# One more wait ahead of a down-projection step: TensorE begins down step 2 of a group only after the group's last gate and up job has ended

## The chip, the cores and the metric

The kernel runs on one core of one Trainium2 chip. The metric is the device time of one execution in microseconds (us), the median over several runs. TensorE (PE in the profile) multiplies matrices and loads their weights (PEld), VectorE (DVE) and ScalarE (ACT) do element-wise work, GpSimd (POOL) does more of it, SyncE (SP) only issues transfers. Engines run their own instruction streams in order and meet at semaphores.

## The reference, cut to what matters

A block on 16,384 tokens (8 sequences of 2048) of 256 features: a layer norm, linear attention with a residual and a second norm, a gated feed-forward network with a third norm, and a ternary-weight gate on the result.

```python
xn = _layernorm(x)
qkv = xn @ Wqkv + bqkv; q, k, v = split(qkv)
qp, kp = elu(q) + 1, elu(k) + 1
kv = einsum('bsd,bse->bde', kp, v)
attn = (qp @ kv) / (qp . sum(kp) + ATTN_EPS)
z = layer_norm(xn + attn, g1, b1)
gate, up = z @ Wg + bg, z @ Wu + bu          # 256 -> 682
ffn = (silu(gate) * up) @ Wd + bd            # 682 -> 256
s = layer_norm(z + ffn, g2, b2)
out = x + s * silu(xn @ ternary(weight).T)
```

## The kernel before, in words

The tokens are cut into 32 groups of 512. An iteration of the main loop works on several groups at once: on group f = i the feed-forward network, on q = i + 1 the attention output, on a = i + 5 the keys and values. Every float is split into a high and a low part, so that one product takes three matmuls: high by high, and the two cross terms (`parts3`).

TensorE's work is a hand-written list of jobs for an iteration, `TENSOR_JOBS` (line 90); `END_JOBS` (line 111) is the list of the last group. The names that matter here are G and U (gate and up of one of five 128-wide slices of the hidden layer, six matmuls with 512 columns each), GU 5 (the remainder of gate and up in one job, six matmuls), D 0 to D 5 (the down product of one slice into the two `d_bank` buffers, twelve matmuls with 256 columns; D 5 has four), K and Q (keys and queries), KV (once in four iterations), N (attention output), B (the ternary product), and XK. The list of a middle iteration ends in `XK 1, XK 2, XK 3, GU 5, D 2, TZ 0, TZ 1, D 3`, where the two TZ jobs are left out for all groups from 1 to 30; it begins with `K 0, D 4, KV 0, KV 1, D 5, K 1, N 0`. So the job GU 5 stands directly ahead of D 2. In the list of the last group D 2 comes ahead of U 4 and of GU 5.

Each job begins with its waits. A job that writes one of the five rotating banks waits first until that bank is free, then for its own inputs. `Dn`, the function of the D jobs, waits for the semaphore `hl`, which VectorE raises when the slice of the hidden layer has its high and low parts. GU 5's last matmul raises the semaphore `GU`. ScalarE waits on it for the silu of the remainder (line 811), and ScalarE's copy of the next group's `zT_h` waits on it too (line 802). The hidden parts lie in a ring of three buffers, `h_h` and `h_l`; ScalarE refills a slot when the D job three slices earlier has ended.

The loops of ScalarE, VectorE and GpSimd have lists of the same kind (lines 93 to 109). VectorE takes K's result in `k_add` (line 1014), the attention output in `attn` (lines 1048 to 1058), the hidden layer in `h_rows` and `h_low` (lines 1095 and 1105), and the down result in `ffn_rows` (line 1117). Its `kv_low` (line 1172) releases job N after job KV.

Of the kernel before, what the change touches and what calls it, by code (L numbers as in the profile page):

```python
# [46 lines left out]
GROUPS = BATCH * SEQ // TOK  # L47
# [165 lines left out]
def build_kernel(nc, x, wqkv, bqkv, wg, bg, wu, bu, wd, bd, g1, b1, g2, b2, wt, out):  # L213
# [10 lines left out]
    with ctx:  # L224
# [3 lines left out]
        def sem(name):  # L228
            return ctx.enter_context(nc.semaphore(name))
# [103 lines left out]
        S = {n: sem("s_" + n) for n in names}  # L333

        def parts3(hi_l, lo_l, hi_r, lo_r):

            return ((hi_l, hi_r), (lo_l, hi_r), (hi_l, lo_r))
# [929 lines left out]
        def _(eng):  # L1267
            def products(dst, pairs, name, first=True, last=True, **kw):

                for n, (left, right) in enumerate(pairs):  # L1270
                    ins = eng.matmul(dst, left, right, start=first and n == 0,  # L1271
                                     stop=last and n == len(pairs) - 1, **kw)
                if name:
                    ins.then_inc(S[name], 1)
# [109 lines left out]
            def Dn(g, c):  # L1384
                eng.wait_ge(S["hl"], HC * g + c + 1)
                if c == 0:
                    eng.wait_ge(S["r2"], PAIRS * g)
                    if g == 0:
                        eng.wait_ge(S["w_dl"], 1)
                        eng.wait_ge(S["w_dt"], 1)  # L1390
                if c == HF:
                    eng.wait_ge(S["ha"], 2 * (g + 1))
                slot = (HF * g + c) % HRING
                for t in range(TILES):
                    s = slice(t * P, (t + 1) * P)
                    if c < HF:
                        pairs = parts3(h_h[:, slot, s], h_l[:, slot, s], wd_h[:, c, :], wd_l[:, c, :])
                    else:
                        pairs = ((ht[:, s], wd_h[:, c, :]),)

                    products(d_bank[t // 2][:, (t % 2) * D:(t % 2 + 1) * D],
                             pairs, "D" if t == TILES - 1 or (g == GROUPS - 1 and c == HF and t % 2) else None, first=c == 0 and t % 2 == 0,
                             last=c == HC - 1, skip_group_check=True)
# [38 lines left out]
            for i in ITERATIONS:  # L1442
                for kind, g, n in schedule(i):
                    if kind == "XK":
                        XK(g, n)
                    elif kind == "D":
                        Dn(g, n)
                    elif kind in setup:
                        setup[kind]()
                    else:  # L1450
                        number = NUMBER[kind, g, n]
                        if number >= RING:
                            stage_, count = freed(*JOBS[number - RING])
                            eng.wait_ge(S[stage_], count)
                        run[kind](g, n, bank[number % RING])
# [24 lines left out]
```

## Time and profile before

| | |
|---|---|
| median of three runs | 1210.11 us (1208.1 to 1210.26) |
| the profiled execution's own time | 1209.84 us |
| its span in the profile | 1208.1 us |
| busy: TensorE matmuls, VectorE, ScalarE, GpSimd | 1187.2, 1079.5, 953.2, 843.7 us |
| mean granted TensorE clock | 0.998 of full |

The busy time of TensorE runs from the start of a matmul to its modelled end, and matmuls overlap: one with 512 columns is shown as 0.39 us long, but the next starts about 0.23 us after it. So the distance between starts is the pace, and the shown duration is what a reader of the result has to wait for. A stretch can have no idle time in the record and still run later than its pace.

### The profile page before, as it was taken

The page shows a single profiled execution, that of the slowest core. Times are in us where ns is not written, and L with a number is a line of the kernel's source. Part 1 is how long each engine was busy: PE and PEld are TensorE (multiplying, and loading weights), DVE is VectorE, ACT ScalarE, POOL GpSimd, SP SyncE. Part 2 cuts the span into 40 slices and gives each one's busy share as a digit, 9 for nine tenths or more (in the row PEclk, how much of TensorE's full clock was granted, in tenths as well). Part 3 has the DMA queues.
Part 4 walks back from the last instruction along what each step waited for, and adds up shares of the span by engine and source line. Part 5 has one row for each costly group of instructions (what it writes and reads, how often), then busy time and mean ns, then how long its engine had stood idle before and what let it go on. Part 6 is the DMA issues. An engine that isn't in the chain of part 4 may idle for free.

```text
span 1208.1 us, 24021 instructions
## 1 busy us (share of the span) xinstructions
PE 1187.2 (98%) x7550; PEld 1067.3 (88%) x7550; DVE 1079.5 (89%) x2467; ACT 953.2 (79%) x1557; POOL 843.7 (70%) x994
## 2 busy tenths in 40 slices
PE   8999999999999999999999999999999999999997
PEld 6889998989988999988989989899988999888886
DVE  6988999999999999999999999999999999777765
ACT  7787888878888888888878888788887878867753
POOL 3443787767787776787757887677886767766676
PEclk9999999999999999999999999999999999999999
DMA  7213432334432334432334432244332343222201
GB/s 216 78 48 88 123 106 70 88 106 123 123 104 72 88 106 123 122 105 73 88 106 122 110 103 83 75 123 123 109 96 67 97 123 105 71 71 63 76 21 36
DMA packets 137523, 115.61 MB, mean 96 GB/s; under 512 B 12339, under 2 KB 122293, under 8 KB 137398
## 3 DMA queue, kind: packets, MB, share of 16 engines
q1 hardware_dynamic: 137398, 114.08, 32.6%
q8 instruction: 62, 1.02, 0.3%
q14 instruction: 63, 0.52, 0.1%
HBM read 67.38 MB, written 46.67 MB: 94 GB/s over the span
## 4 chain that ended last, share of the span: by engine, by line
PE 52%; DVE 21%; ACT 11%; issue 9%; DMA 3%; POOL 2%; SPq 1%; DVEq 0%; ACTq 0%; POOLq 0%
PE bank L1271 36%; PE d_bank L1271 11%; PE xk_bank L1271 5%; DVE st L922 3%; DVE bank L1095 3%; ACT rz L695 3%; DVE rz L1054 2%; DVE h_l L1105 2%; DMA xa<-z_turned 2%; DMA z_turned<-xa 2%; ACT h_h L695 1%; DVE zT_l L1085 1%; ACT ku L695 1%; POOL norm L569 1%; ACT hs L695 1%
## 5 line engine op out<-in xcount | busy, mean ns | idle before, releaser
L1271 PE MATMUL bank<-zT_h,wgu_h 128*128 128x512 f32 x704 | 275.1, 391 | 1.1 <-DVE rz L1054 1.1
L1271 PE MATMUL bank<-zT_l,wgu_h 128*128 128x512 f32 x704 | 275.1, 391 | 0.0
L1271 PE MATMUL bank<-zT_h,wgu_l 128*128 128x512 f32 x704 | 275.0, 391 | 0.0
L695 ACT ACTIVATE rz<-rz,norm 128x256 f32<-128x256 f32 x252 | 140.5, 595 | 53.6 <-DVE norm L1131 53.6
L569 POOL TENSOR_TENSOR norm<-ve,consts 128x4 f32<-128x4 f32 x64 | 72.9, 1139 | 154.7 <-DVE ve L933 154.5
L1271 PE MATMUL d_bank<-wd_h,h_h 128*128 128x256 f32 x640 | 179.4, 280 | 0.1
L1271 PE MATMUL d_bank<-wd_h,h_l 128*128 128x256 f32 x640 | 179.2, 280 | 0.0
L1271 PE MATMUL d_bank<-wd_l,h_h 128*128 128x256 f32 x640 | 179.2, 280 | 0.0
L1095 DVE SCALAR_TENSOR_TENSOR bank<-bank,hb,hs 128x512 f32<-128x512 f32 x160 | 117.9, 754 | 53.6 <-ACT hs L695 41.9
L695 ACT ACTIVATE h_h<-bank 128x512 fp32r<-128x512 f32 x160 | 95.7, 598 | 80.7 <-DVE bank L1095 80.4
L1271 PEld LDWEIGHTS bank<-zT_l,wgu_h 128*128 128x128 f32 x704 | 132.2, 188 | 28.1
L1271 PEld LDWEIGHTS bank<-zT_h,wgu_h 128*128 128x128 f32 x704 | 132.4, 188 | 25.6 <-DVE rz L1054 3.9
L695 ACT ACT_TABLE_LOAD x116 | 148.8, 1283 | 4.0 <-POOL wd_l L678 1.2
L1271 PEld LDWEIGHTS bank<-zT_h,wgu_l 128*128 128x128 f32 x704 | 132.2, 188 | 20.1
L592 POOL TENSOR_TENSOR ksum<-ksum,kp 128x256 f32<-128x256 f32 x120 | 108.3, 903 | 45.6 <-DVE kp L1021 42.3
L695 ACT ACTIVATE hs<-bank,hb 128x512 f32<-128x512 f32 x192 | 128.3, 685 | 13.2 <-PE bank L1271 12.2
L1105 DVE TENSOR_TENSOR h_l<-bank,h_h 128x512 fp32r<-128x512 f32 x160 | 110.0, 687 | 23.7 <-ACT h_h L695 17.5
L1271 PEld LDWEIGHTS d_bank<-wd_h,h_h 128*128 128x128 f32 x640 | 120.2, 188 | 3.1 <-DVE h_l L1105 0.5
L1271 PEld LDWEIGHTS d_bank<-wd_h,h_l 128*128 128x128 f32 x640 | 120.2, 188 | 2.7
L1271 PEld LDWEIGHTS d_bank<-wd_l,h_h 128*128 128x128 f32 x640 | 122.2, 191 | 0.0
L642 POOL TENSOR_TENSOR rz<-rz,g1b 128x256 f32<-128x256 f32 x128 | 118.1, 933 | 0.0
L602 POOL TENSOR_TENSOR rz<-rz,g2b 128x256 f32<-128x256 f32 x124 | 90.6, 741 | 34.9 <-ACT rz L695 34.9
(163 smaller groups left out, 3571.8 us busy)
## 6 DMA issues: line engine op xcount, KB each, us to landing
xq<-in_L_attn_x_dram SPq DMA_DIRECT2D x32, 512.0 KB, 5.9
xa<-in_L_attn_x_dram SPq DMA_DIRECT2D x31, 512.0 KB, 3.9
out_dram<-rz SPq DMA_DIRECT2D x31, 512.0 KB, 5.0
z_turned<-xa SPq DMA_DIRECT2D x120, 128.0 KB, 3.3
xa<-z_turned SPq DMA_DIRECT2D x30, 512.0 KB, 4.1
turned<-xa SPq DMA_DIRECT2D x108, 128.0 KB, 2.4
xa<-turned SPq DMA_DIRECT2D x27, 512.0 KB, 3.9
rz<-in_L_attn_Wg_dram SPq DMA_DIRECT2D x1, 640.0 KB, 5.7
```

The lines of the kernel that those rows point to most:

```text
L569: eng.tensor_tensor(dst, ve[:, k, :], neg_half[:, 0:1].to_broadcast([P, TILES]), ALU.pow).then_inc(S[f"rs{k}"], 1)
L592: eng.tensor_tensor(ksum[:, slot, :], ksum[:, slot, :], part, ALU.add).then_inc(S["ks"], 1)
L602: eng.tensor_tensor(row_, row_, g2b[:, :], ALU.mult).then_inc(S["a"], 1)
L642: eng.tensor_tensor(row_, row_, g1b[:, :], ALU.mult).then_inc(S["zg"], 1)
L695: return eng.activation(out_, in_, func, **kw).then_inc(S[name], 1)
L922: eng.bn_stats(st[:, k, t, :], rows).then_inc(S[f"bn{k}"], 1)
L1054: eng.scalar_tensor_tensor(out=rz[:, g % RZ, t, :], in0=num[:, 0:D], scalar=den[:, n % 2, 1:2], in1=rz[:, g % RZ, t, :], op0=ALU.mult, op1 ...
L1085: eng.tensor_tensor(to, source, high.bitcast(f32), ALU.subtract).then_inc(S["zTl"], 1)
L1095: eng.scalar_tensor_tensor(out=hidden(g, c)[0:rows, :], in0=up, scalar=hb[0:rows, HC + c:HC + c + 1], in1=hs[0:rows, n % 2, :], op0=ALU.ad ...
L1105: eng.tensor_tensor(h_l[:, slot, :], hidden(g, c)[:, :], h_h[:, slot, :].bitcast(f32), ALU.subtract).then_inc(S["hl"], 1)
L1271: ins = eng.matmul(dst, left, right, start=first and n == 0, stop=last and n == len(pairs) - 1, **kw)
```

## The change

In `Dn` a third wait is put in for step c = 2 of every group but the last. It wants the semaphore `GU` at g + 1, so that group g's remainder job has ended. No instruction is moved and none is taken away; the step now has the wait for `hl` first and the wait for `GU` second.

```diff
@@ -1390,6 +1390,8 @@
                         eng.wait_ge(S["w_dt"], 1)
                 if c == HF:
                     eng.wait_ge(S["ha"], 2 * (g + 1))
+                if c == 2 and g < GROUPS - 1:
+                    eng.wait_ge(S["GU"], g + 1)
                 slot = (HF * g + c) % HRING
                 for t in range(TILES):
                     s = slice(t * P, (t + 1) * P)
```

The place in TensorE's stream, once in each of the 31 groups from 0 to 30. Ahead of it stand the last two matmuls of GU 5, behind it the first three of D 2.

```order
 L1271 MATMUL bank<-zT_h,wgu_l 128x512
 L1271 MATMUL bank<-zT_l,wgu_h 128x512
-L1271 MATMUL d_bank<-wd_h,h_h 128x256 [waits s_hl]
+L1271 MATMUL d_bank<-wd_h,h_h 128x256 [waits s_GU,s_hl]
 L1271 MATMUL d_bank<-wd_h,h_l 128x256
 L1271 MATMUL d_bank<-wd_l,h_h 128x256
```

Nothing moved: the first matmul of D 2 has one more semaphore to wait for, and that semaphore is raised by the matmul right above it. VectorE, ScalarE, GpSimd and SyncE have the same rows as before.

## Rows read from the trace of the kernel before

**Rows 1.** The page: span, busy time, and the chain that ended last by engine
```profile
span 1208.1 us, 24021 instructions
PE 1187.2 (98%) x7550; PEld 1067.3 (88%) x7550; DVE 1079.5 (89%) x2467; ACT 953.2 (79%) x1557; POOL 843.7 (70%) x994
...
PE 52%; DVE 21%; ACT 11%; issue 9%; DMA 3%; POOL 2%; SPq 1%; DVEq 0%; ACTq 0%; POOLq 0%
```

**Rows 2.** Timeline (start us, length us) at D 2 of group 13
```profile
574.45 0.39 PE L1271 MATMUL bank<-zT_l,wgu_h 128*128 128x512 f32 x1
...
574.68 0.28 PE L1271 MATMUL d_bank<-wd_h,h_h 128*128 128x256 f32 x1
...
574.80 0.28 PE L1271 MATMUL d_bank<-wd_h,h_l 128*128 128x256 f32 x1
```

**Rows 3.** Timeline: GU 5's last matmul of group 14, and ScalarE's silu
```profile
610.16 0.39 PE L1271 MATMUL bank<-zT_l,wgu_h 128*128 128x512 f32 x1
...
610.59 0.69 ACT L695 ACTIVATE hs<-bank,hb 62x512 f32<-62x512 f32 x1
```

**Rows 4.** Timeline at N 0 of group 12, whose late wait is not its first
```profile
474.20 0.43 DVE L1172 TENSOR_TENSOR kv_l<-bank,kv_h 128x258 fp32r<-128x258 f32 x1
...
474.75 0.19 PEld L1271 LDWEIGHTS bank<-kv_h,qp_h 128*128 128x128 f32 x1 [0.24 <-issue]
474.78 0.36 PE L1271 MATMUL bank<-kv_h,qp_h 128*128 128x258 f32 x1
...
474.97 0.28 PE L1271 MATMUL bank<-kv_h,qp_l 128*128 128x258 f32 x1
```

**Rows 5.** Timeline at Q 1 of group 13, whose late wait is its first
```profile
487.67 0.68 DVE L1105 TENSOR_TENSOR h_l<-bank,h_h 128x512 fp32r<-128x512 f32 x1
...
488.40 0.19 PEld L1271 LDWEIGHTS bank<-xT_h,wq_h 128*128 128x128 f32 x1 [0.34 <-DVE h_l L1105]
488.40 0.50 PE L1271 MATMUL bank<-xT_h,wq_h 128*128 128x512 f32 x1
...
488.75 0.40 PE L1271 MATMUL bank<-xT_h,wq_l 128*128 128x512 f32 x1
```

**Rows 6.** Timeline: first matmul of D 2 in groups 0, 1, 14, 15, 26
```profile
102.52 0.28 PE L1271 MATMUL d_bank<-wd_h,h_h 128*128 128x256 f32 x1
...
138.17 0.28 PE L1271 MATMUL d_bank<-wd_h,h_h 128*128 128x256 f32 x1
...
610.39 0.28 PE L1271 MATMUL d_bank<-wd_h,h_h 128*128 128x256 f32 x1
...
649.07 0.28 PE L1271 MATMUL d_bank<-wd_h,h_h 128*128 128x256 f32 x1
...
1048.40 0.28 PE L1271 MATMUL d_bank<-wd_h,h_h 128*128 128x256 f32 x1
```

**Rows 7.** Timeline: first matmul of KV 0, and D 5 behind KV 1
```profile
616.30 0.28 PE L1271 MATMUL bank<-wv_h,kv_h 128*128 128x256 f32 x1
...
618.08 0.48 PE L1271 MATMUL d_bank<-wd_h,ht 128*128 128x256 f32 x2
```

**Rows 8.** Waits of 102 to 1048 us by engine: us in total, times, longest
```profile
PEld bank L1271 <- DVE h_l L1105: 4.6, 15, 0.7
...
PEld bank L1271 <- DVE rz L1054: 2.5, 10, 0.6
PEld bank L1271 <- issue: 2.3, 8, 0.5
```

**Rows 9.** Timeline: K 1's last matmul of group 19, VectorE's `k_add`
```profile
582.10 0.28 PE L1271 MATMUL bank<-wk_l,xT_h 128*128 128x256 f32 x1
...
582.83 0.67 DVE L1014 TENSOR_TENSOR kp<-bank,bk1b 128x512 f32<-128x512 f32 x1
```

**Rows 10.** One stretch: us, busy per engine, granted clock (PEclk) behind POOL
```profile
102.50:1048.40 945.90, 944.52 (x6077) 855.55 (x6076) 884.19 (x1990) 779.43 (x1264) 701.81 (x805) 1.00 0.34 100
```

**Rows 11.** Timeline: weight load of U 0 in group 29, after a wait
```profile
1122.03 0.19 PEld L1271 LDWEIGHTS bank<-zT_h,wgu_h 128*128 128x128 f32 x1 [1.33 <-DVE rz L1054]
```

## The prediction

> **What bounds the kernel now.** I read the page's busy times first: TensorE is busy 98% of the span, VectorE 89% [rows 1]. Busy time alone does not show who sets the pace, because shown matmuls overlap, so I went to the distances between starts. D 2 begins once in an iteration, and its first matmul is a good clock: 102.52, 138.17 and so on to 1048.40 us [rows 6]. The shortest distance is 35.65 us, and it holds when all of TensorE's jobs follow each other without a break. If all 26 iterations between 102.52 and 1048.40 were like it, with 1.78 us more for each of the six that hold the KV jobs (616.30 to 618.08 [rows 7]), the stretch would take 26 x 35.65 + 6 x 1.78 = 937.6 us. It takes 945.9. So TensorE sets the pace, but loses about 8.3 us to stalls, 0.3 us an iteration. They are not spread evenly. Taking the same bases, 16 of the 26 distances are at most 0.23 us over, about 0.9 us together; the other ten are 0.42 to 1.34 us over. The longest is 610.39 to 649.07 [rows 6], a KV iteration.
>
> What TensorE waits for in those is VectorE: `h_low`, `attn`, and the late `kv_low` that the view of waits books as "issue" [rows 8]. So VectorE's chain is second and close behind, and that matters for the sum.
>
> The two chains meet at one place in each iteration. GU 5's last matmul starts at 610.16 and ends at 610.55; ScalarE's silu of it starts at 610.59, 0.04 us later [rows 3]. That is one of 23 such pairs (groups 3 to 25); the gap is 0.04 in most and 0.19 us at most. From there ScalarE and VectorE go their own way until they release TensorE again in K, N, Q or U.
>
> **The price of one pause.** Today D 2 follows GU 5 without a break: starts at 574.45, 574.68 and 574.80 [rows 2], with D 2's first weights loaded under the last matmul of GU 5. With the wait, TensorE must see that matmul end. I take the steps one by one.
>
> End of the matmul: 0.39 us after its start [rows 2]. From the end of a releaser to TensorE's next weight load: VectorE's `kv_low` ends at 474.63, the load starts at 474.75, which is 0.12; the matmul starts 0.03 after the load and the second matmul 0.19 after the first, at 474.97 [rows 4]. When the late wait is the first of its job it is quicker: `h_low` ends at 488.35 and load and matmul both start at 488.40, 0.05 later, though the second matmul comes 0.35 after the first where the usual pace is 0.23 [rows 5]. The new wait stands behind the one for `hl`, which is like the job N, whose late wait is also behind another; I take that case. Then D 2's second matmul, the first that is back on the normal pace, starts at 574.45 + 0.39 + 0.12 + 0.03 + 0.19 = 575.18 in place of 574.80. One pause costs 0.38 to 0.39 us. By the quicker case it would be 0.39 (end) + 0.05 (release) + 0.12 (0.35 - 0.23, the second matmul's delay) - 0.23 (the distance of today) = 0.33. No row shows TensorE waiting for itself; the other end of a wait for TensorE, ScalarE's 0.04 us [rows 3], is no longer than the 0.05 seen from VectorE, so I see no reason for a dearer signal, and allow 0.45 as the upper bound.
>
> There are 31 pauses, one for each group from 0 to 30: 31 x 0.39 = 12.1 us. Behind the waiting matmul stand, in TensorE's stream, D 2, D 3 and all of the next iteration. The instructions of the other engines are unchanged, and what they wait for from D 2 (the ring of hidden slots, the banks) is used many microseconds later. The wait itself is fulfilled the moment the drained matmul is signalled; there is nothing else to wait for.
>
> **What of it is hidden.** The pause lies behind GU 5, and the chain ScalarE - VectorE starts from GU 5, not from D 2. So in an iteration where TensorE later stalls for VectorE, TensorE only arrives later at a place where it would have stood anyway, and the pause costs nothing up to the length of the stall. This needs VectorE not to be late in turn. The tightest place that I found where it takes something from TensorE behind the pause is `k_add` of K 1: K 1's last matmul starts at 582.10 and ends at 582.38, `k_add` starts at 582.83, 0.45 later [rows 9]. Less the 0.04 of the signal there is a margin of 0.41 us, and the pause of 0.39 just fits in. I take the hand-overs of the other jobs (K 0, D 5, N, G, U) as looser.
>
> Ten iterations have stalls of over 0.39 us, so they hide ten pauses. The 1.33 us gap ahead of U 0 in group 29 [rows 11] hides an eleventh. That is 11 x 0.39 = 4.3, and of the small stalls I count 0.4 of the 0.9 us. Hidden: 4.7 us, as much as 12 whole pauses. Net: 12.1 - 4.7 = 7.4 us. The profiled execution took 1209.84 us, so 1217.2; the median of the runs is 0.27 above it, which gives **1217.5 us**.
>
> **The rivals.**
>
> *Nothing is hidden.* If the margin at `k_add` does not hold, or VectorE's chain moves along with TensorE for another reason, the stalls stay and every pause counts. For it: the margin is only 0.02 us larger than the pause. Against it: at N 0 of group 12 the stall ends with VectorE's `kv_low` [rows 4], on a chain that began at GU 5, ahead of the pause. Time: 1210.1 + 12.1 = 1222.2.
>
> *The pause is smaller.* With the weights of D 2 loaded while the wait is open, the first matmul would come 0.43 us after the last one's start and the next at the normal pace, 0.20 us lost: (31 - 12) x 0.20 = 3.8, or 1213.9. Against it: in both waits that I read the load starts only after the releaser [rows 4, 5]. The middle case of 0.33 gives 19 x 0.33 = 6.3, or 1216.4, and belongs to my forecast. The Trainium skill, page "TensorE: Matmul & The Clock Gate", section "Step-by-step: what each phase is for", says that the engine pulls the next weight load ahead of matmuls in flight; if a load could also pass a wait, this rival would hold. The rows show the pulling ahead at D 2 today (the load of its first weights is not on the path [rows 2]), and none past a wait.
>
> *Not slower: VectorE and ScalarE set the period.* If their chain from one GU 5 to the next took as long as TensorE's, TensorE would have at least 0.39 us to spare in every iteration, and the pauses would go into it: 1210.1, at most 1211. It decides from a spare time of 0.39 us in each of the 26. For it: VectorE is busy for 884 of 945.9 us [rows 10], and the chain that ended last has only 52% of TensorE in it [rows 1]. Against it: 16 of 26 distances have no more than 0.23 us to spare, and silu waits for GU 5 in each [rows 3]. So the pause must show in those 16.
>
> *The clock falls.* The stretch ran at a granted clock of 1.00, which is 2.4 GHz [rows 10], and the 1.33 us gap [rows 11] did not lower it. If a short pause in each iteration did bring the lower level, 1.2 GHz, for no more than D 2, its twelve matmuls of 0.12 us (574.68 to 574.80 [rows 2]) would take 1.4 us more: 31 x 1.4 = 43 us on top of the 7.4, or 1261. The Trainium skill, on the same page, section "A second HAM failure mode: psum-queue depth-cycling", says that frequent short idle spots between groups of matmuls can make the clock swing. The trace disagrees so far: TensorE's load unit sat idle 33 times in that stretch for a release [rows 8], and the clock stayed at 1.00 [rows 10].
>
> **How the numbers follow.** Forecast, with most stalls hiding their pauses: 0.62 (1215 to 1220). Nothing hidden or almost nothing: 0.15. Small pause: 0.14. Not slower: 0.04. Clock: 0.01. The rest, 0.04, is a dearer pause: (31 - 12) x 0.45 = 8.6, or 1218.7, and 1224 with nothing hidden. The range from **1213.5 to 1222.5** takes in the small pause and nothing hidden, and leaves out the last three. A measurement of this kernel can tell 0.2%, 2.4 us, from no change. Slower by more: 0.95. Within: 0.04. Faster by more: 0.01, since a wait adds no speed anywhere and only the shared timing of the other engines could turn it.
>
> **What would show it right or wrong.** Each D 2 should start 0.53 to 0.55 us after the start of GU 5's last matmul, not 0.23, with an idle spot of TensorE or of its weight load there and the load starting after the release. The shortest distance between D 2 starts should be 36.03 us, not 35.65. The stalls ahead of N, Q and U should shrink or go, and the total of TensorE's stalls outside the new place should fall from 8.3 us to about 4. If those stalls keep their size, "nothing is hidden" is right; if the shortest distance stays at 35.65, the third rival is. A granted clock under 0.99 in the middle would speak for the fourth.

## The result, and the profile after

The changed kernel takes 1214.54 us (median of five runs, 1213.48 to 1214.94); the kernel before takes 1210.11 us (median of five, 1208.06 to 1210.66) beside it. The ratio is 1.0045, with an interval of [1.0034, 1.0057]: slower by 4.4 us. Measured a second time (e7 below), the change gave 1215.11 us against 1208.84 of the kernel before, ratio 1.0055 [1.0043, 1.0067], or 6.3 us, where 1213.0 to 1215.5 had been expected. The forecast was 1217.5 us with a range from 1213.5 to 1222.5. Sign and range hold; the middle was 2.4 to 3 us too high.

The page of the kernel after, for [rows 1]: span, busy time, the chain that ended last by engine, and the group of D's first products (busy us, mean ns, then idle time ahead and what ended it).

```profile
span 1213.0 us, 24052 instructions
PE 1189.7 (98%) x7550; PEld 1064.2 (88%) x7550; DVE 1082.9 (89%) x2467; ACT 952.9 (79%) x1557; POOL 839.2 (69%) x994
...
PE 69%; DVE 13%; ACT 9%; issue 6%; POOL 1%; DMA 1%; SPq 0%; DVEq 0%; ACTq 0%; POOLq 0%
...
L1271 PE MATMUL d_bank<-wd_h,h_h 128*128 128x256 f32 x640 | 181.2, 283 | 4.7 <-PE bank L1271 1.4
```

The busy shares tell almost nothing of the change: TensorE is at 98% as before, although it now stands still 31 times. The chain tells no more, though it looks as if it did. TensorE has 69% of it where it had 52% [rows 1], but in the pages of e1 and e10 below, neither of which has a pause, it has 37% and 73%.

The timeline of the kernel after at D 2 of group 13 answers [rows 2] (start us, length us, idle time before and its releaser).

```profile
578.58 0.39 PE L1271 MATMUL bank<-zT_l,wgu_h 128*128 128x512 f32 x1
579.00 0.69 ACT L695 ACTIVATE hs<-bank,hb 62x512 f32<-62x512 f32 x1 [0.36 <-PE bank L1271]
579.08 0.19 PEld L1271 LDWEIGHTS d_bank<-wd_h,h_h 128*128 128x128 f32 x1 [0.54 <-DVE h_l L1105]
579.11 0.36 PE L1271 MATMUL d_bank<-wd_h,h_h 128*128 128x256 f32 x1 [0.15 <-PE bank L1271]
579.31 0.28 PE L1271 MATMUL d_bank<-wd_h,h_l 128*128 128x256 f32 x1
```

D 2's first matmul starts 0.53 us after GU 5's last one, in place of 0.23, and the second 0.20 later, in place of 0.12 (medians over the 31 places: 0.538 and 0.192). The weight load starts at 579.08, 0.11 us after the matmul that it waits for has ended. That end is modelled; the distance from start to start is not. The releaser named for the load, `h_low`, is not the true one: the same place is booked to "issue" in other groups, and it has no gap in e1 below, where D 2 waits for `h_low` as well. ScalarE's silu starts where it always did, right at the end of GU 5.

The first matmul of D 2 in groups 0, 13, 14 and 26 of the kernel after, for [rows 6].

```profile
103.34 0.36 PE L1271 MATMUL d_bank<-wd_h,h_h 128*128 128x256 f32 x1
...
579.11 0.36 PE L1271 MATMUL d_bank<-wd_h,h_h 128*128 128x256 f32 x1 [0.15 <-PE bank L1271]
...
615.15 0.36 PE L1271 MATMUL d_bank<-wd_h,h_h 128*128 128x256 f32 x1
...
1053.48 0.36 PE L1271 MATMUL d_bank<-wd_h,h_h 128*128 128x256 f32 x1 [0.15 <-PE bank L1271]
```

From 579.11 to 615.15 are 36.04 us, where an iteration with no stall took 35.65. That is one pause more, to the hundredth. It is the usual distance: 15 of the 26 are 36.03 or 36.04 (in e7 16 of them are 36.07). Three are shorter, 35.92 and twice 35.80, in iterations whose matmuls with 256 columns follow each other faster (see e6). From 103.34 to 1053.48 are 950.1 us, where the kernel before took 945.9: 26 pauses have cost 4.3 us, not 26 x 0.39 = 10.1.

The rest is in the waits of the weight loads, 102 to 1053 us of the kernel after, for [rows 8] (us in total, times, longest).

```profile
PEld d_bank L1271 <- issue: 9.2, 17, 0.5
PEld d_bank L1271 <- DVE h_l L1105: 4.9, 9, 0.5
PEld bank L1271 <- DVE h_l L1105: 2.4, 8, 0.4
PEld bank L1271 <- DVE rz L1054: 1.1, 5, 0.3
PEld bank L1271 <- issue: 0.3, 1, 0.3
```

The two rows on `d_bank` are the new pauses. The three on `bank` are the stalls that were there already: 3.8 us together, where they were 9.4 [rows 8]. So 5.6 us of old stalls have gone.

**One iteration read closely.** In group 14's, the longest of before (610.39 to 649.07, 38.68 us [rows 6]), TensorE stood at N 0 for `kv_low`, here in the kernel before:

```profile
620.49 0.19 PEld L1271 LDWEIGHTS bank<-kv_h,qp_h 128*128 128x128 f32 x1 [0.54 <-issue]
```

In the kernel after, the only waits of the weight loads from 615.00 to 653.00 are these:

```profile
615.12 0.19 PEld L1271 LDWEIGHTS d_bank<-wd_h,h_h 128*128 128x128 f32 x1 [0.54 <-issue]
628.90 0.19 PEld L1271 LDWEIGHTS bank<-zT_h,wgu_h 128*128 128x128 f32 x1 [0.17 <-DVE rz L1054]
638.26 0.19 PEld L1271 LDWEIGHTS bank<-xT_h,wq_h 128*128 128x128 f32 x1 [0.35 <-DVE h_l L1105]
...
653.42 0.36 PE L1271 MATMUL d_bank<-wd_h,h_h 128*128 128x256 f32 x1
```

The wait at N 0 is gone, and the iteration, 615.15 to 653.42, is 38.27 us long: shorter than before, with the pause in it.

**The clock** in the same stretch, for [rows 10]:

```profile
102.50:1048.40 945.90, 941.89 (x6051) 848.90 (x6050) 883.13 (x1986) 775.25 (x1258) 694.32 (x802) 1.00 0.34 99
```

The granted clock is 1.00, the level of 2.4 GHz, as before, with some 26 pauses in it.

### The profile page after: what moved, and what is told of

The parts are those of the page before. It is cut to its first block, busy times and chain, and to the rows that moved or that the text cites. A ratio compares the mean times of both kernels' runs of the same rounds, so it can differ in the third digit from the quotient of the medians.

```text
span 1213.0 us, 24052 instructions
## 1 busy us (share of the span) xinstructions
PE 1189.7 (98%) x7550; PEld 1064.2 (88%) x7550; DVE 1082.9 (89%) x2467; ACT 952.9 (79%) x1557; POOL 839.2 (69%) x994
## 4 chain that ended last, share of the span: by engine, by line
PE 69%; DVE 13%; ACT 9%; issue 6%; POOL 1%; DMA 1%; SPq 0%; DVEq 0%; ACTq 0%; POOLq 0%
PE bank L1271 48%; PE d_bank L1271 15%; PE xk_bank L1271 5%; ACT rz L695 2%; DVE bank L1095 2%; DVE st L922 2%; DVE h_l L1105 1%; DVE rz L1054 1%; DVE zT_l L1085 1%; ACT hs L695 1%; ACT ku L695 1%; ACT qp L695 1%; ACT h_h L695 1%; ACT kp_h L695 1%; ACT qp_h L695 1%
## 5 line engine op out<-in xcount | busy, mean ns | idle before, releaser
L592 POOL TENSOR_TENSOR ksum<-ksum,kp 128x256 f32<-128x256 f32 x120 | 105.3, 878 | 46.3 <-DVE kp L1021 43.0
L1271 PEld LDWEIGHTS d_bank<-wd_h,h_h 128*128 128x128 f32 x640 | 120.1, 188 | 18.8 <-issue 10.9
```

What stands on the lines that cost most here:

```text
L592: eng.tensor_tensor(ksum[:, slot, :], ksum[:, slot, :], part, ALU.add).then_inc(S["ks"], 1)
L1271: ins = eng.matmul(dst, left, right, start=first and n == 0, stop=last and n == len(pairs) - 1, **kw)
```

## The experiments

**How they are read.** For each kernel's profile I took the starts of TensorE's matmuls from D 2 of group 0 to D 2 of group 30 and compared each distance with the pace in which matmuls follow each other: 0.227 us with 512 columns, 0.118 with 256. What is over the pace from GU 5 to D 2's second matmul (in one kernel, from XK 3 to GU 5's second; in one, at D 3 as well) I call pauses; every other distance that is over by more than 0.03 us, stalls; the sum of all that is left, pace. The three columns add up to the stretch, up to one constant of 1054.1 us. All kernels here compute everything.

| kernel | pauses | stalls | pace | stretch, us | runs, median us | ratio to before |
|---|---|---|---|---|---|---|
| before | 0 | 10.3 | +3.6 | 1068.1 | 1208.8 to 1210.1 | |
| e1, an old wait | 0 | 8.6 | +3.5 | 1066.3 | 1207.74 | 0.9987 [0.9978, 0.9995] |
| the change | 11.6 | 4.7 | +1.8 | 1072.2 | 1214.54 | 1.0045 [1.0034, 1.0057] |
| e7, the change again | 11.6 | 3.5 | +3.5 | 1072.7 | 1215.11 | 1.0055 [1.0043, 1.0067] |
| e2, pause ahead of GU 5 | 10.4 | 10.9 | -0.7 | 1074.8 | 1219.23 | 1.0084 [1.0070, 1.0098] |
| e3, two pauses | 23.2 | 2.7 | -2.2 | 1077.8 | 1219.79 | 1.0092 [1.0078, 1.0106] |
| e6, own wait first | 9.7 | 6.6 | -3.1 | 1067.4 | 1209.17 | 1.0004 [0.9995, 1.0013] |
| e4, ahead of stalls | 4.3 | 5.9 | +3.2 | 1067.5 | 1209.33 | 1.0002 [0.9994, 1.0011] |
| e5, the other groups | 7.4 | 7.3 | +3.6 | 1072.4 | 1214.64 | 1.0045 [1.0033, 1.0058] |
| e10, fourth matmul | 0 | 8.2 | +3.4 | 1065.8 | 1208.15 | 0.9991 [0.9982, 1.0000] |
| e9, fifth matmul | 3.0 | 8.9 | -2.1 | 1064.0 | 1207.92 | 0.9989 [0.9980, 0.9998] |
| e12, e9 again | 3.0 | 9.0 | -1.5 | 1064.7 | 1207.26 | 0.9991 [0.9983, 0.9999] |
| e11, fifth, second | 4.8 | 5.4 | +3.0 | 1067.3 | 1210.06 | 1.0012 [1.0004, 1.0020] |

The stalls of one kernel vary by 1 to 2 us between executions: the kernel before, e1 and e10 have no drain to wait for and show 10.3, 8.6 and 8.2. The first of them has the single stall of 1.33 us [rows 11] that the other two lack; e5 has one like it. In the pace column only the differences between kernels mean something: N's matmuls, with 258 columns, are 0.120 us apart and make up a part of it in all.

### e1: the instruction without its wait

```diff
+                if c == 2 and 0 < g < GROUPS - 1:
+                    eng.wait_ge(S["GU"], g)
```

> The same second wait ahead of D 2, but for the GU of the group before, which ended an iteration earlier: the wait instruction stays, the draining goes. Theory (the cost is the drained matmul): 1210.1 us within 0.7, D 2 starting 0.23 us after GU 5's last matmul as before. Rival (the instruction or the loss of the early weight load costs): 31 x 0.05 to 0.2 us more, 1211.7 to 1216.

Measured: 1207.74 us, ratio 0.9987 [0.9978, 0.9995]. The timeline of e1 at the same place:

```profile
575.23 0.39 PE L1271 MATMUL bank<-zT_l,wgu_h 128*128 128x512 f32 x1
575.23 0.19 PEld L1271 LDWEIGHTS d_bank<-wd_h,h_h 128*128 128x128 f32 x1
575.45 0.28 PE L1271 MATMUL d_bank<-wd_h,h_h 128*128 128x256 f32 x1
575.57 0.28 PE L1271 MATMUL d_bank<-wd_h,h_l 128*128 128x256 f32 x1
```

The weights are loaded under GU 5 and D 2 follows at the normal pace, as in [rows 2]. The extra wait instruction costs nothing when it was fulfilled long ago. All of the cost is in waiting for the matmul right ahead. The time is 1.7 us under that of before beside it (1209.45), and under the expected 1210.1 within 0.7; e10 below comes out the same way. Why a kernel with a wait more should be 0.1% faster, no run here shows.

### e2: the same pause on the other side of the hand-over

```diff
             def GU(g, c, dst):
+                if g + LEAD < GROUPS:
+                    eng.wait_ge(S["XK"], TILES * (g + LEAD + 1))
+                elif g < GROUPS - 1:
+                    eng.wait_ge(S["G"], 2 * HF * (g + 1))
                 gate_or_up(g, 2 * HF * P, dst, "GU")
```

D 2 has no wait of its own here; GU 5 waits for the job ahead of it, so that ScalarE and VectorE get GU 5 late as well.

> One pause an iteration as in the change, but one job earlier: GU 5, not D 2, waits until the job right ahead of it has ended (XK 3, or U 4 where there is no XK). The prediction's step (the VectorE chain starts at GU 5, so only a pause behind GU 5 is hidden in the stalls) gives the full price: a pause of 0.39 to 0.43 us, 31 of them, 12 to 13.3 us, so 1222 to 1223.5. The theory that I hold now (VectorE and ScalarE run on with their own lateness, and any pause of TensorE's in the iteration lets them catch up) gives about what the change gave, plus 31 x 0.04 for the slightly dearer pause: 1214.5 to 1216.5.

Measured: 1219.23 us, ratio 1.0084 [1.0070, 1.0098], 4 to 5 us more than the change, although one pause is smaller: 0.385 us from XK 3 to GU 5 in place of 0.118, and 0.306 to the next in place of 0.227, 0.35 us together. That lies between the two expectations: over the 1214.5 to 1216.5 of a pause that hides as well as the change's, and under the 1222 to 1223.5 of the full price, which reckoned with a pause of 0.39 to 0.43 and an unchanged pace. The timeline of e2:

```profile
578.08 0.28 PE L1271 MATMUL xk_bank<-kp_l,xn_h 128*128 128x256 f32 x1
578.43 0.19 PEld L1271 LDWEIGHTS bank<-zT_h,wgu_h 128*128 128x128 f32 x1 [0.28 <-issue]
578.46 0.47 PE L1271 MATMUL bank<-zT_h,wgu_h 128*128 128x512 f32 x1
578.76 0.39 PE L1271 MATMUL bank<-zT_h,wgu_l 128*128 128x512 f32 x1
```

And its waits from 102 to 1053 us:

```profile
PEld bank L1271 <- issue: 9.0, 32, 0.3
PEld bank L1271 <- DVE h_l L1105: 7.6, 24, 0.7
PEld bank L1271 <- DVE rz L1054: 2.5, 10, 0.9
```

The pauses are in the first row. The waits for `h_low` have not shrunk, as they did after the change (to 2.4), but grown from 4.6 [rows 8] to 7.6. By the starts of matmuls the stalls are 10.9 us, where they are 8.2 to 10.3 without a pause: nothing is hidden. (The stretch of e2 is only 2.1 to 2.6 us longer than that of the change, since the pace gave 2.5 to 4.2 back and this profiled execution, 1217.22 us, was 2 us under e2's median; both hide a part of the difference, and neither touches the stalls.) So what hides a pause is that it lies behind the place where ScalarE and VectorE are fed; the same pause ahead of it moves both chains.

### e3: a second pause behind D 2

```diff
+                if c == 2 and g < GROUPS - 1:
+                    eng.wait_ge(S["GU"], g + 1)
+                if c == 3 and g < GROUPS - 1:
+                    eng.wait_ge(S["D"], HC * g + 3)
```

> The change, and a second pause of the same kind: D 3 waits until D 2 has ended, in groups 0 to 30. By its rows a pause behind a matmul of 256 columns costs 0.28 + 0.12 + 0.03 + 0.19 - 0.12 - 0.12 = 0.38 us. Theory (the first pause has used up nearly all stalls, 8.3 us of them at the start): the second is paid in full, 31 x 0.38 = 11.8 us over the change, 1226.3, at least 1225. Rival (each pause hides in stalls that VectorE makes anew): 1219 to 1222.

Measured: 1219.79 us, ratio 1.0092 [1.0078, 1.0106], 5.3 us over the change where a full second set of pauses was expected to give 11.8. The expectation failed, and not by the pause itself, in the timeline of e3 at D 3:

```profile
581.61 0.28 PE L1271 MATMUL d_bank<-wd_l,h_h 128*128 128x256 f32 x1
582.01 0.19 PEld L1271 LDWEIGHTS d_bank<-wd_h,h_h 128*128 128x128 f32 x1 [0.32 <-issue]
582.04 0.36 PE L1271 MATMUL d_bank<-wd_h,h_h 128*128 128x256 f32 x1
582.24 0.28 PE L1271 MATMUL d_bank<-wd_h,h_l 128*128 128x256 f32 x1
```

It is 0.43 us from matmul to matmul in place of 0.12, and 0.20 to the next: 0.39, the same price as at D 2. The table shows where the rest went: 11.6 us of pauses more than in e7, but only 2.7 us of stalls are left to hide anything in (0.8 less), and 5.7 us came back in the pace. That term was not in any of my theories. It is taken up with e6. In the same D 3 it can be seen to begin: the matmuls start at 582.24, 582.36, 582.47, 582.59, and from the sixth on at 582.70, 582.82, 582.93, 583.04, 583.15, so 0.1133 us apart in place of 0.118.

### e6: the same wait, put first

```diff
             def Dn(g, c):
+                if c == 2 and g < GROUPS - 1:
+                    eng.wait_ge(S["GU"], g + 1)
                 eng.wait_ge(S["hl"], HC * g + c + 1)
```

> The change with its two waits in the other order: first GU, then hl. Theory (the late wait is quicker to release TensorE when it is the job's first, 0.33 against 0.386 us a pause): D 2 starts 0.45 us after GU 5's last matmul in place of 0.54, its second matmul comes 0.22 us later, and the kernel takes 31 x 0.056 = 1.7 us less than the change, 1212.8. Rival (the order doesn't matter): 1214.5.

Measured: 1209.17 us, ratio 1.0004 [0.9995, 1.0013], the same as before. It was expected near 1212.8: a miss. The pause is there, in the timeline of e6, and it is the quick case of the prediction (0.33 us), as in [rows 5]:

```profile
575.55 0.39 PE L1271 MATMUL bank<-zT_l,wgu_h 128*128 128x512 f32 x1
575.99 0.19 PEld L1271 LDWEIGHTS d_bank<-wd_h,h_h 128*128 128x128 f32 x1 [0.48 <-PE bank L1271]
575.99 0.38 PE L1271 MATMUL d_bank<-wd_h,h_h 128*128 128x256 f32 x1
576.22 0.28 PE L1271 MATMUL d_bank<-wd_h,h_l 128*128 128x256 f32 x1
```

GU 5 to D 2 takes 0.45 us, the next matmul 0.22: 0.324 us over the pace by the medians, 9.7 us in the stretch. What pays for them is the pace. Twelve matmuls with 256 columns, the length of a K or D job, take either 1.413 us (0.1178 each, shown as 281 ns long) or 1.360 us (0.1133 each, shown as 276), at a granted clock of 1.00 in both. The rows by tile, first of the kernel after and then of e6 (ns min/median/max):

```profile
L1271 PE MATMUL bank<-wk_h,xT_l x256: 276/281/288, 11.1 to 1024.8; 128*128 128x256 f32 x128
```

```profile
L1271 PE MATMUL bank<-wk_h,xT_l x256: 276/276/283, 10.3 to 1019.8; 128*128 128x256 f32 x128
```

Most K jobs of e6 run at the faster pace, most of the kernel after at the slower. Of the 210 jobs K and D with twelve matmuls, 35 are at the faster pace in the kernel before, 40 in e1, 68 after the change, 58 in e7, 146 in e6 (counted by the length of the whole job; where the line is drawn moves these counts by up to 3). D 3, directly behind D 2, ends at the faster pace in all 31 groups of e2, e3, e6, e9 and e12, in 4 after the change, and in 1, the last, in each of the others.

### e4 and e5: the pause in some of the groups

```diff
+                if c == 2 and g in (4, 6, 10, 14, 15, 18, 21, 22, 24, 26, 28):
+                    eng.wait_ge(S["GU"], g + 1)
```

This is e4: groups in whose iterations the profiled execution of before had stalled. The choice is not clean. Group 2 had 0.6 us of stalls and is left out, and 21, 24 and 28 have none in e1 and e10. e5 has the wait in the other 20 groups (`g not in` the same list).

> The change's wait in 11 groups only: 4, 6, 10, 14, 15, 18, 21, 22, 24, 26 and 28, those after whose D 2 the profiled execution of the kernel before had a stall of over 0.35 us in the same iteration. Theory of the prediction (a pause hides in the stall that follows it in the iteration, up to its own length): 0 us, 1209.5 to 1210.5. Rival (the stalls come and go from execution to execution and the choice of groups means little): 11 of 31 pauses of the change, 11 x 0.386 = 4.2 less a third of the 7 us given back = 2.0, so 1211 to 1212.

> The other half: the wait in the 20 groups from 0 to 30 that the run before leaves out. Theory of the prediction (no stalls of size follow there, so hardly anything is hidden): 20 x 0.386 = 7.7 us, less 0.4, so 1217. Rival (VectorE's lateness is worked off over several iterations, and these pauses hide too): 20 of 31 parts of 4.4, 2.9 us, so 1212 to 1214.

Measured: e4 1209.33 us, ratio 1.0002 [0.9994, 1.0011]; e5 1214.64 us, ratio 1.0045 [1.0033, 1.0058], 5.7 us over the 1208.91 of before beside it. Eleven pauses cost 0.4 us in the runs, twenty cost 5.7, each within 1 to 1.5 us. e4 is what the prediction's theory gave. e5 is not: one pause costs 0.29 us there, not 0.39, and the time is 2.4 us under the expected 1217.

The stalls by group, from the starts of matmuls, show more than the sums (us in the profiled execution, from D 2 of a group to the next D 2):

| kernel | iterations of the eleven groups | of the other twenty |
|---|---|---|
| before, e1, e10: no pause | 9.3, 6.4, 6.6 | 0.9, 2.2, 1.6 |
| e4: pauses in the eleven | 3.2 | 2.7 |
| e5: pauses in the other twenty | 6.8 | 0.4 |

Where the pauses are the stalls shrink, and where they are not they stay. So what an iteration hides does not depend on its neighbours. Against e1 and e10 e4 hides 3.2 to 3.5 of its 4.3 us of pauses, and e5 1.2 to 1.8 of its 7.4, where I had expected 0.4. That figure came from one profiled execution. Group 2, which belonged to the other half by its stall, hides 0.3 of it, and in e1 and e10 there are stalls of 0.4 to 0.7 us in iterations of the twenty (12, 13, 20, 23) where the kernel before had none: they come and go, and a pause hides in them too.

### e9, e10, e11 and e12: a wait for an earlier matmul of the same job

A semaphore of its own, `gm`, is raised by the fifth matmul of GU 5 (n == 4; e10: by the fourth, n == 3). TensorE then does not have to see the last matmul of GU 5 end.

```diff
             def GU(g, c, dst):
...
+                    if n == 4:
+                        ins.then_inc(S["gm"], 1)
...
             def Dn(g, c):
+                if c == 2 and g < GROUPS - 1:
+                    eng.wait_ge(S["gm"], g + 1)
                 eng.wait_ge(S["hl"], HC * g + c + 1)
```

GU's loop over its six matmuls is written out in `GU` for this (line 1387 in the rows). e11 has the same wait behind the one for `hl`; e12 is e9 unaltered.

> No pause to speak of: GU 5's fifth matmul of six raises a semaphore of its own, and D 2 waits for that first and for hl second, as the variant with the two waits turned round did for the sixth. By the rows the fifth ends 0.16 us after the sixth begins and its release 0.05 us later, so D 2 can start 0.22 us after the sixth, as ever. Theory (that variant paid 0.32 us a pause and got about 0.28 us an iteration back because the jobs of 256 columns behind it ran at 0.1133 in place of 0.1178 us a matmul, and this comes from a weight load that waits first in its job): D 3 takes 1.36 us, and the kernel is faster than before, by 5 to 7 us, 1203 to 1205, if the second matmul's 0.1 us delay is small. Rival (the faster pace comes from the drained array itself): D 3 takes 1.41 us and the time is 1209 to 1212.

> The same with GU 5's fourth matmul, whose release is there by the time that the sixth starts, so that nothing is held back. Theory (the waiting weight load makes the pace, if it is still held at all when TensorE reaches it): between before and the variant with the fifth, 1203 to 1210. Rival (no pause, no faster pace): as before, 1209 to 1210.

> The variant with the semaphore of GU 5's fifth matmul, but with the two waits in the change's order: hl first, the fifth matmul second. Theory (a wait that is not the first of its job makes TensorE start 0.15 us after the release, the weight load 0.12 us after): the fifth ends 0.16 us after the sixth begins, so D 2 starts 0.31 us after the sixth in place of 0.23, a pause of 0.08 and 0.08 more for the second matmul, 31 x 0.16 = 5 us before anything is hidden, and D 3 stays at the slow pace of 1.41 us as in the change: 1209 to 1212. Rival (the order doesn't matter for what comes behind): D 3 at 1.36 us, 1206 to 1208.

> The variant with the fifth matmul's semaphore first and hl second once more, unaltered, for the size of its gain: its profile showed 4 us less between the first and the last D 2 of the middle groups, its runs 0.1%. If the profile is right about the runs without it: 0.9965 of before. If the gain is small: 0.9985 to 0.9995.

Measured: e9 1207.92 (0.9989), e12 1207.26 (0.9991), e10 1208.15 (0.9991), e11 1210.06 (1.0012), with the intervals of the table. In e9 the faster pace came and the time did not, so neither of its two expectations holds: D 3 takes 1.36 us, and the kernel is not at 1203 to 1205. e10 does what its rival said, no pause and no faster pace. e11 lies in its range of 1209 to 1212, with a slow D 3, and e12 shows the small gain. The timeline of e9:

```profile
574.20 0.39 PE L1387 MATMUL bank<-zT_l,wgu_h 128*128 128x512 f32 x1
574.42 0.19 PEld L1271 LDWEIGHTS d_bank<-wd_h,h_h 128*128 128x128 f32 x1 [0.25 <-PE bank L1387]
574.43 0.38 PE L1271 MATMUL d_bank<-wd_h,h_h 128*128 128x256 f32 x1
574.64 0.28 PE L1271 MATMUL d_bank<-wd_h,h_l 128*128 128x256 f32 x1
```

and of e11, with the order of the two waits turned:

```profile
575.94 0.39 PE L1387 MATMUL bank<-zT_l,wgu_h 128*128 128x512 f32 x1
576.22 0.19 PEld L1271 LDWEIGHTS d_bank<-wd_h,h_h 128*128 128x128 f32 x1 [0.32 <-issue]
576.25 0.36 PE L1271 MATMUL d_bank<-wd_h,h_h 128*128 128x256 f32 x1
576.45 0.28 PE L1271 MATMUL d_bank<-wd_h,h_l 128*128 128x256 f32 x1
```

In e9 the matmul waited for ends at 573.97 + 0.39 = 574.36, and D 2 starts at 574.43, which is also when it would have started without a wait, 0.23 after the last of GU 5. Only its weights come late, so the second matmul is 0.21 us behind the first in place of 0.12: 0.10 us lost, 3.0 in the stretch. In e11 the matmul waited for ends at 575.72 + 0.39 = 576.11, the load starts 0.11 us later and the matmul 0.14: 0.31 us from GU 5 to D 2 and 0.20 to the next, 0.16 us lost, 4.8 in the stretch. So a late wait in the second place costs 0.06 to 0.07 us more than in the first, from a twin pair of kernels. In e10 the fourth matmul has ended by the time that TensorE comes to the wait, D 2's second matmul follows at 0.117 us, and the kernel behaves as before.

e9 and e12 have the faster pace (137 and 131 of the 210 jobs), e10 and e11 don't (40 and 52). In the profiles this is worth 4.9 to 5.6 us of pace against e1 and e10, 1 to 2 us net behind the pauses and stalls that it brings; in the runs e9 and e12 are 0.1% below the kernel before, and so are e1 and e10, which lack it. So none of them is shown to be better than another, and I don't offer one as an improvement.

## Why the prediction was right, and where it was off

**TensorE sets the pace, the waits can be counted: right.** The usual distance of D 2 starts grew from 35.65 to 36.03 us (36.07 in e7); 36.03 was forecast. It was forecast for the shortest one, though, and that is 35.80, in the two iterations of the faster pace.

**The price of one pause, 0.38 to 0.39 us: right, and so was its build.** 0.39 for the end of the matmul, 0.11 to the weight load, 0.03 to the matmul, 0.20 to the next, against 0.39, 0.12, 0.03 and 0.19. By the modelled end of the matmul, TensorE sees its own work end no sooner and no later than VectorE's [rows 4]. That the place of the late wait in its job decides between the dear and the quick case, which I took from two different jobs [rows 4, 5], is shown by turning the order of the waits at one place: 0.386 against 0.324 us (the change and e6), 0.16 against 0.10 (e11 and e9). The rival of a weight load that passes the wait is out. The Trainium skill, page "TensorE: Matmul & The Clock Gate", section "Step-by-step: what each phase is for", says that the load of the next weights can be pulled ahead of matmuls in flight; the trace agrees as long as the wait is fulfilled (e1, load at 575.23 with the matmul), and shows no load ahead of an open one (579.08, after the end at 578.97).

**Pauses in iterations with stalls are hidden: the mechanism right, its size a little under.** The forecast was 4.7 us hidden. The stalls fell by 5.6 us, by the waits and by the starts of matmuls alike, in the first pair of profiles, and in the second by 4.7 to 5.1 (3.5 against the 8.2 and 8.6 of e10 and e1). e2 shows the reason that the prediction gave, the place behind the hand-over at GU 5; e4 shows the same group by group. What was missed is that the other iterations hide a part as well (e5): I had counted 0.4 us of small stalls there, from one execution, and it is 1.2 to 1.8. One reading was off without harm: the longest of the ten stalls is 38.68 - 37.43 = 1.25 us by [rows 6, 7], not 1.34.

**The margin at `k_add` of K 1: it did not hold everywhere, and it did not matter.** The timeline of the kernel after, for [rows 9]:

```profile
586.61 0.28 PE L1271 MATMUL bank<-wk_l,xT_h 128*128 128x256 f32 x1
...
586.93 0.69 DVE L1014 TENSOR_TENSOR kp<-bank,bk1b 128x512 f32<-128x512 f32 x1
```

`k_add` follows K 1's end by 0.04 us, where it was 0.45; 0.04 is what a wait that ends last leaves. The prediction took the 0.45 of one place for the tightest. Over the 26 iterations with a K 1 the gap was 0.32 to 1.34 us before, with a median of 0.48, and in five of them it was too small for a pause of 0.39 and the signal. After the change it is 0.04 in 8 iterations, and in 13 in e7: VectorE does wait there. But that brought no stalls back. Outside the KV iterations VectorE's first `attn` starts 10.74 us after GU 5's last matmul before, 10.76 after and 10.75 in e7 (medians). e3 goes further: there `k_add` waits in 17 of 26 iterations and the first `attn` comes at 10.92, and still only 2.7 us of stalls are left. So the condition that the prediction set, a margin of 0.41 against a pause of 0.39, is not what kept "Nothing is hidden" away; that the forecast held with it broken in some iterations was luck. Where VectorE makes up the lost tenths before TensorE needs it was not traced.

**The step that was off: that nothing else in TensorE's stream changes.** The sum has a term for pauses and one for stalls and takes the pace of all other matmuls as fixed. In the profile of the change 68 jobs of 210 ran at the faster pace in place of 35, worth 1.8 us. In e7 it was 58, but the pace column is that of e1 and within 0.1 of before's, because the distances in N and in the gate and up jobs grew by about what the K and D jobs gained. The sum of e7 against e1 and e10 is 11.6 of pauses less 4.9 of stalls, 6.7 us, close to the 7.4 of the forecast. So of the 3 us by which the first median lies under 1217.5, by the profiled execution about 1 is stalls hidden beyond the forecast, about 2 is this pace, and 0.5 is that the pauses came to 11.6 and not 12.1. In e6 and e3 the same term was 6.7 us (against before) and 5.7 us (against e7), and made both expectations fail. The base moves too: the two medians of before, 1210.11 and 1208.84, are 1.3 us apart, and from the second one the change costs 6.3 us, 1.1 less than forecast.

**The other rivals.** VectorE and ScalarE do not set the period: the usual distance moved with the pause. The clock did not fall. The Trainium skill, on the same page, section "A second HAM failure mode: psum-queue depth-cycling", warns of micro-idles between groups of matmuls; 31 pauses here (mean granted clock 0.997 in the profiled execution, 0.998 before), and 62 in e3 (0.998), left it where it was, so no run here shows that effect. One execution of e4 that was not profiled has 0.948; it took 1209.38 us, e4's median within 0.1, so whatever it was cost nothing.

## What to carry to other kernels

A wait of TensorE for its own last matmul cost 0.39 us here, and 0.32 as the first wait of its job; for one that ended long ago it costs nothing, so an order that one engine must keep with itself is best tied to a job that is already over. What a pause costs in the end is decided by its place: behind the job that feeds the other engines, it is paid out of the stalls that these would have caused, as far as there are any; ahead of it, the other engines come late as well and nothing is hidden. Where a wait is late by nature, try it as the first wait of its job, and compare the pace of the matmuls behind it before crediting the wait alone.

## What the runs showed of the hardware that I had not expected

**Two paces at one clock.** Matmuls with 256 columns follow each other at 0.1178 or at 0.1133 us, 4% apart, at a granted clock of 1.00 in both. The pace can change within a job: in e6 the D 2 of group 13 is at about 0.118 at first and at 0.1133 (576.69, 576.80, 576.91) from its sixth matmul, and D 3 and K 0 keep it. XK's are always at the slower one. Which pace holds depends on how TensorE came to D 2: with a late wait in the first place (e6, e9, e12) or a pause one job earlier (e2) it is the faster behind D 2; with none, with one in the second place (the change, e11) or with one in some groups, mostly the slower. But the place of the wait is not the rule. In e3, with two pauses both in the second place, D 3 changes to the faster pace from its sixth matmul on in all 31 groups, and K 0, D 4, D 5 and K 1 keep it; and after the change, with the same pause in every group, D 2 turns fast in three groups (7, 19, 23) and not in the others. What makes the choice was not settled, and neither was whether all of it lasts outside a profiled execution: e9's profiled execution was the shortest of its eleven (1205.55 against a median of 1207.92), though e6's was its median.

**The first wait is cheaper than the second.** From the modelled end of the matmul waited for to the next matmul it is 0.05 to 0.06 us when the late wait stands first (e6; the 0.07 of e9 is also the usual distance from GU 5), and 0.14 us when it stands second (the change, e11). In the first case the second matmul comes 0.10 us late, in the other 0.08. Why the place matters, no run here shows.
